# Spreading gate rows over the partitions by DMA instead of by a matmul and a copy

## What is computed

```python
def _more_forward(x, Wg, bg, W1, b1, W2, b2):
    cur = x
    for r in range(R):                                   # R = 4
        flat = cur.reshape(-1, h)                        # 1024 x 128
        logits = flat @ Wg[r] + bg[r]                    # 1024 x 4
        vals, idx = jax.lax.top_k(logits, TOPK)          # TOPK = 2
        w = jax.nn.softmax(vals, axis=-1)
        cw = jnp.sum(jax.nn.one_hot(idx, E, dtype=flat.dtype) * w[..., None], axis=1)
        hmid = jax.nn.gelu(jnp.einsum('nh,ehf->enf', flat, W1) + b1[:, None, :])
        y = jnp.einsum('enf,efh->enh', hmid, W2) + b2[:, None, :]
        out = jnp.einsum('ne,enh->nh', cw, y)
        cur = cur + out.reshape(b, s, h)
    return cur
```

## Time and profile before

| | |
|---|---|
| median of 3 runs | 539.47 us (538.99 to 543.11) |
| profiled execution, its own time | 534.68 us |
| its span (first to last instruction) | 532.9 us |
| granted TensorE clock over the span | 0.935 |
| busy PE, DVE, ACT, POOL | 462.3, 351.4, 323.8, 133.1 us |
| ACT's two gelus of a chunk (L665, L666), 128 each | 702 and 677 ns |
| DVE's split of a chunk (L1063), 128 | 688 ns |
| DMA traffic, mean | 30 GB/s |

### The profile page before, as it was taken

How to read it: one execution, slowest core, us unless ns; L and a number is a source line. 1 busy time by engine, 2 the same in 40 slices (tenths; PEclk the granted TensorE clock), 3 DMA queues, 4 the chain that set the end, 5 groups by cost and what they waited for, 6 DMA issues and landing times.

```text
span 532.9 us, 8485 instructions
## 1 busy us (share of the span) xinstructions
PE 462.3 (87%) x2692; PEld 354.8 (67%) x2692; DVE 351.4 (66%) x967; ACT 323.8 (61%) x620; POOL 133.1 (25%) x195
## 2 busy tenths in 40 slices
PE   3768998988994798579998877999999999999995
PEld 2447776755741587447777755878788787878783
DVE  4376766777469665546778746858585867777653
ACT  2446666632255334034666537898988989898892
POOL 7070000112145200123645330021111221111121
PEclk9978999997898799856999987999999999999999
DMA  8911111000400000001111000000000000000001
GB/s 293 369 35 26 31 28 29 16 1 1 159 1 1 0 1 2 0 20 30 33 31 31 22 0 1 1 2 1 0 0 0 0 0 0 0 0 1 1 1 39
DMA packets 12754, 16.07 MB, mean 30 GB/s; under 512 B 4008, under 2 KB 11304, under 8 KB 12080
## 3 DMA queue, kind: packets, MB, share of 16 engines
q1 hardware_dynamic: 12288, 14.79, 8.8%
q10 hardware_dynamic: 432, 0.85, 0.4%
HBM read 10.92 MB, written 0.52 MB: 21 GB/s over the span
## 4 chain that ended last, share of the span: by engine, by line
PE 57%; DVE 12%; issue 9%; ACT 8%; DMA 6%; SPq 5%; POOL 3%; ACTq 0%; POOLq 0%; DVEq 0%
SPq L295 5%; DMA bigr<-qk 5%; PE ps L1200 5%; PE ps L1515 4%; PE ps L1516 4%; PE ps L1514 4%; PE ps L1533 4%; PE ps L1532 4%; PE ps L1531 4%; PE ps L1245 3%; PE ps L1212 3%; POOL xnT L442 2%; ACT big L526 2%; PE ps L1522 2%; ACT qk L477 2%
## 5 line engine op out<-in xcount | busy, mean ns | idle before, releaser
L1063 DVE TENSOR_TENSOR bigr<-ps,bigr 128x512 fp32r<-128x512 f32 x128 | 86.2, 688 | 56.7 <-ACT ps L666 56.7
L526 ACT ACTIVATE big<-ps 128x512 f32<-128x512 f32 (+1 forms) x128 | 68.5, 547 | 58.2 <-PE ps L1212 56.1
L665 ACT ACTIVATE bigr<-ps,b 128x512 fp32r<-128x512 f32 x128 | 89.8, 702 | 3.0
L666 ACT ACTIVATE ps<-ps,b 128x512 f32<-128x512 f32 x128 | 86.6, 677 | 0.0
L442 POOL TENSOR_TENSOR xnT<-xnT,big 128x512 f32<-128x512 f32 x32 | 41.4, 1294 | 160.9 <-DVE big L1070 160.9
L1200 PE MATMUL ps<-bigr,qk 128*128 128x256 f32 (+1 forms) x224 | 55.1, 329 | 12.5 <-DMA bigr<-qk 11.1
L808 DVE TENSOR_REDUCE nmax<-ps 128x2 f32<-128x512 f32 x64 | 42.8, 688 | 18.4 <-PE ps L1200 17.6
L1212 PE MATMUL ps<-qk,bigr 128*128 128x256 f32 (+1 forms) x256 | 51.2, 285 | 1.0 <-ACT big L526 0.7
L1200 PEld LDWEIGHTS ps<-bigr,qk 128*128 128x128 f32 x224 | 35.7, 200 | 24.6 <-DMA bigr<-qk 15.0
L801 DVE CUSTOM_DVE_ANT_0 masked<-ps,later 128x128 f32<-128x128 f32 (+1 forms) x128 | 39.1, 352 | 18.8 <-PE ps L1200 18.7
L1514 PE MATMUL ps<-k1hi,w1hi 128*128 128x512 f32 x128 | 51.5, 402 | 0.0
(11 more groups left out here) (198 smaller groups left out, 852.6 us busy)
## 6 DMA issues: line engine op xcount, KB each, us to landing
bigr<-qk SPq DMA_DIRECT2D x128, 32.0 KB, 1.9
wi<-in_wi SPq DMA_DIRECT2D x1, 2048.0 KB, 7.7
wo<-in_wo SPq DMA_DIRECT2D x1, 2048.0 KB, 12.2
big<-in_sel SPq DMA_DIRECT2D x1, 1024.0 KB, 8.6
wo<-in_w SPq DMA_DIRECT2D x1, 1024.0 KB, 4.8
wi<-in_w SPq DMA_DIRECT2D x1, 1024.0 KB, 6.9
x<-in_x SPq DMA_DIRECT2D x1, 512.0 KB, 5.4
ctxT<-in_ctxT ACTq DMA_DIRECT2D x1, 512.0 KB, 5.2
```

The lines of the kernel that those rows point to most:

```text
L526: act.activation(prob[:, h % 8, c], ps[:, 2 + h % 2, c], ACT.Exp, scale=DH ** -0.5).then_inc(s(L + "_exp"), 1)
L665: act.activation(ghi[:, u % 2, c, :], ps[:, c, :], ACT.Gelu_apprx_tanh, bias=b1[:, u % E1, c:c + 1])
L666: act.activation(ps[:, c, :], ps[:, c, :], ACT.Gelu_apprx_tanh, bias=b1[:, u % E1, c:c + 1]).then_inc(s("ff1_gel"), 1)
L1063: v.tensor_tensor(glo[:, u % 2, c, :], ps[:, c, :], ghi[:, u % 2, c, :].bitcast(f32), ALU.subtract).then_inc(s("ff1_glo"), 1)
```

## The change

`cwT` becomes a plain f32 tile on 4 partitions, one for each expert. The matmul `spread` with its selector (`sel_er`, `sel_e`) and the copy `spread_weights` are gone; so are the three DVE instructions that rounded and split the gates, and the transposes take `cw` itself. In their place SP waits, for each half in each round, until ACT has written the four rows to `cwT`, and issues four DMAs. Each reads one row of 512 f32 (2 KB) on one partition 128 times, and writes it to the 128 partitions of `cwb[:, u, :]`: 256 KB a DMA, 4 a half, 8 halves, 32 in all. `combine` waits for the DMA of its own unit (semaphores `ff1_cwb0` to `ff1_cwb7`). What PE waits for at u = 3 and u = 7 stays.

```diff
-        cwT = sb("cwT", [P, 2, HALF], f32r)
-        sel_er = sb("sel_er", [P, E1, P], f32r)
+        cwT = sb("cwT", [E1, 2, HALF])
...
+            for Hf in range(2 * R1):
+                sp.wait_ge(s("ff1_ctev"), 1 + Hf + 1)
+                for e in range(E1):
+                    u = Hf % 2 * E1 + e
+                    sp.dma_start(cwb[:, u, :], cwT[e:e + 1, Hf % 2, :].unsqueeze(1).broadcast_to([1, P, HALF])
+                                 ).then_inc(s("ff1_cwb%d" % u), 16)
...
-            def spread_weights(U, u):
-
-                act.wait_ge(s("ff1_bcd"), U + 1)
-                act.activation(cwb[:, u % 8, :], ps[:, 6, :], ACT.Copy).then_inc(s("ff1_cwb"), 1)
...
-                act.activation(cwT[0:2 * E1, hf, :], ps[0:2 * E1, bank, :], ACT.Copy).then_inc(s("ff1_ctev"), 1)
+                act.activation(cwT[:, hf, :], ps[0:E1, bank, :], ACT.Copy).then_inc(s("ff1_ctev"), 1)
...
-                own.step(v.scalar_tensor_tensor(cw[:, 0:m], dif[:, 0:m], 1.0, selh[:, 0:m], ALU.add, ALU.mult))
-                own.step(v.tensor_copy(cwr[:, 0:m], cw[:, 0:m]))
-                c3, r3 = (a[:, 0:m].rearrange("p (n e) -> p n e", e=E1) for a in (cw, cwr))
-                own.mark(v.tensor_copy(cwhl[:, :, 0:E1], r3.bitcast(f32)))
-                v.tensor_tensor(cwhl[:, :, E1:2 * E1], c3, r3.bitcast(f32), ALU.subtract).then_inc(s("ff1_cwd"), 1)
+                v.scalar_tensor_tensor(cw[:, 0:m], dif[:, 0:m], 1.0, selh[:, 0:m], ALU.add, ALU.mult
+                                       ).then_inc(s("ff1_cwd"), 1)
...
-            def combine(U, u):
+            def combine(U, u, r):
                 dve.wait_ge(s("ff1_dn"), 2 + U + 1)
-                dve.wait_ge(s("ff1_cwb"), 1 + U + 1)
+                dve.wait_ge(s("ff1_cwb%d" % u), 16 * (r + 1))
...
-                    last = pe.transpose(ps[0:2 * E1, bank, n * P:n * P + P], cwhl[:, n, :], ident[:, :])
+                    last = pe.transpose(ps[0:E1, bank, n * P:n * P + P], cw[:, n * E1:n * E1 + E1], ident[:, :])
...
-            def spread(U, u):
-
-                u = u % (2 * E1)
-                pe.wait_ge(s("ff1_cwb"), U + 1)
-                pe.matmul(ps[:, 6, :], sel_er[:, u % E1, :], cwT[:, u // E1, :], start=True, stop=True
-                          ).then_inc(s("ff1_bcd"), 1)
```

More of the change, by code:

```diff
@@ L195, in decoder_kernel @@
         cw = sb("cw", [P, NT * E0])
-        cwr = sb("cwr", [P, NT * E0], f32r)
-        cwhl = sb("cwhl", [P, 4, 2 * E1])
-        sel_e = sb("sel_e", [2 * E1, E1, P])
         oNT = sb("oNT", [P, TPB, P])
@@ L283, in _ @@
             load("ff1", tie1[:, :, :], w["tie1"].partition_broadcast(P))
-            load("ff1", sel_e[:, :, :], w["sel_e"])
             load("ff0", wi0[:, :, :, :], w["wi0"])
@@ L325, in _ @@
             pool.wait_ge(s("const"), 6)
-            pool.memset(cwT[:, :, :].bitcast(f32), 0.0).then_inc(s("ff1_zero"), 1)
-            pool.memset(sel_er[:, :, :].bitcast(f32), 0.0).then_inc(s("ff1_zero"), 1)
             pool.memset(first_row[:, :], 0.0).then_inc(s("at1_row"), 1)
@@ L454, in _ @@
             act.sem_inc(s("ff1_ctev"), 1)
-            act.sem_inc(s("ff1_cwb"), 1)
             for name, dst, src in (("ctx", ctxT[:, :], "ctxT"), ("ctx", wctx[:, :, :], "wctx"),
@@ L684, in round_ @@
                     if not (last and u == 7):
-                        spread_weights(U0 + u + 1, u + 1)
                         gelus(U0 + u + 1, u + 1)
@@ L693, in _ @@
             gelus(0, 0)
-            act.wait_ge(s("ff1_zero"), 2)
             gate_rows(0, 0, 6)
             evacuate_xnT("ff1", 1, 5)
-            spread_weights(0, 0)
             with act.Fori(0, R1 - 1) as r:
@@ L1017, in constants @@
             def constants():
-                dve.wait_ge(s("ld_ff1"), 6 * 16)
-                dve.wait_ge(s("ff1_zero"), 2)
-                own.mark(v.tensor_copy(sel_er[0:2 * E1, :, :], sel_e[:, :, :]))
+                dve.wait_ge(s("ld_ff1"), 5 * 16)
                 own.mark(v.tensor_scalar(maskf[:, :], mask_i[:, :], 0, None, ALU.not_equal))
@@ L1095, in round_ @@
                         add_experts(0)
-                    combine(U0 + u, u)
+                    combine(U0 + u, u, r)
                     if u == 0:
@@ L1106, in _ @@
             dve.wait_ge(s("ln_xnT"), ln("ff1", 2) + 2)
-            per = 2 * 1 + 2 * (9 + 3)
+            per = 2 * 1 + 2 * 9
             with dve.Fori(0, R1 - 1) as r:
@@ L1488, in gate_rows @@
                 for n in range(4):
-                    last = pe.transpose(ps[0:2 * E1, bank, n * P:n * P + P], cwhl[:, n, :], ident[:, :])
+                    last = pe.transpose(ps[0:E1, bank, n * P:n * P + P], cw[:, n * E1:n * E1 + E1], ident[:, :])
                 last.then_inc(s("ff1_ct"), 1)
             def first_logits():
-                pe.wait_ge(s("ld_ff1"), 6 * 16)
+                pe.wait_ge(s("ld_ff1"), 5 * 16)
                 pe.wait_ge(s("ln_xnT"), ln("ff1", 2) + 1)
@@ L1554, in round_ @@
                     if not (last and u == 7):
-                        spread(U0 + u + 1, u + 1)
                         up(U0 + u + 1, u + 1)
@@ L1575, in _ @@
             pe.wait_ge(s("ff1_ctev"), 2)
-            spread(0, 0)
             pe.wait_ge(s("xa1_res"), TPB + TPB * B)
@@ L1615, in shape_constants @@
         c[n] = (np.arange(E)[None, :] < np.arange(E)[:, None]).astype(f)
-    c["sel_e"] = np.ascontiguousarray(np.broadcast_to(
-        (np.arange(2 * E1)[:, None] % E1 == np.arange(E1)[None, :])[:, :, None], (2 * E1, E1, P))).astype(f)
     return c
```

## The result

The changed kernel takes 652.23 us in the median of 4 runs (649.43 to 654.87), against 540.96 us for the kernel before in the same comparison; the ratio is 1.2055, with a 95% interval of 1.1974 to 1.2136. The forecast was 656 us, range 610 to 748. The profiled execution took 649.43 us, its span is 647.7 us.

The account below looks back on a forecast made before the run. PE bounds the last stage before, the new DMAs after: first rows 329.98, issue 0.59, start and completion 1.9, 32 x 9.7 = 310.4, tail 6.2, outside 1.8, median 4.8 give 655.7, predicted 656 us (range 610 to 748).

Parts of the forecast that it names:

- What bounds the kernel: Last stage: PE is the bound, busy 119.96 of 120 us at full clock, while the DMA engines move nothing.
- the DMA's price: Each new 256 KB DMA reads one partition at 26.9 GB/s, so it takes 9.7 us.
- the halved rate of the key copies: SBUF copies between 32 partitions: 14.6 to 15.1 GB/s per engine, about half the loads' rate, suggesting two engines share one way.
- the bound from below: For one new DMA's time: the store of x moves the same 256 KB from 128 partitions, landing in 2.3 us.
- The queue is always full: SP's queue in the last stage: four DMAs take 38.8 us against PE's 23.7 a half, so 32 run gapless, 310 us.
- The sum: Whole kernel: last landing at 642.9, span 649.1, with 1.8 us outside 650.9, plus 4.8 for the median: 655.7 us.
- The clock: PE in the last stage: clock may fall to 0.5, giving 678 us; a mixture off the path expected; chance 0.12.
- SP's issue: SP's queue: about 0.59 us to issue a DMA, 2.4 us for four; landings about 12, 21, 31, 41 us.
- What the removal brings: PE loses 32 matmuls: 1.1 us a half, 8.2 us over thirty slots, plus 1.1 in the prologue, 9.3 us together.
- the rival "hidden": Last stage: DMAs under 5.9 us each are hidden, leaving only removed work; 530 us, 1.7% faster; chance 0.12.

Follow-up runs that it names:

- the kernel with no spreading: Against the kernel before: spreading DMAs and semaphores left out, combine multiplies with a constant weight tile; 536.04 us, ratio 0.9946; in a second comparison 534.58 us, 0.9900.
- rows on 32 partitions: The change, but each gate row stands on 32 partitions, each read four times by the DMA; 536.22 us, ratio 0.9923 to the kernel before.
- 4 apart: The change, but each DMA reads four partitions lying 4 apart (32e, +4, +8, +12); 537.16 us, ratio 0.9923 to the kernel before.
- through HBM: The change, but SP writes the four rows to an HBM buffer and reads them from there; 536.18 us, ratio 0.9903 to the kernel before.
- 64 destinations: The change, but each DMA writes only 64 of the 128 destination partitions; 534.33 us, ratio 0.9872 to the kernel before.
- the 8 matmuls in the gap: Eight matmuls into unused bank 4 before up(1), added to the 32-partition kernel (533.90 us, 0.9852; again 534.84, 0.9894) and the kernel without spreading (533.22 us, 0.9839).

## Why the prediction was right, and where it was off

**What bounds the kernel, and the DMA's price: right, and shown.** The step that decided was the price of one DMA that reads one partition. I put it at 9.7 us; it is 9.6 to 9.8. The row that pointed to it, the halved rate of the key copies, did point to the right thing: with the way to a group of partitions as the narrow place, four neighbours stay slow, and four that lie apart do not; and an engine moves 24.5 GB/s where each has a group of its own, but 14.4 where sixteen read 32 partitions, which are eight such groups. The figure itself was a choice between rows: by 29.2 GB/s it would have been 9.0 us and 633 us in all, by 20.8 12.6 us and 748, and no row showed that 26.9 was the one to take. To that extent the closeness of the number is luck; the mechanism is not. The store's 2.3 us, the bound from below, is of the order of what a DMA takes once it reads 32 partitions or HBM (landings of 4.8 and 3.8 us with four issued together).

**The queue is always full: right.** The DMA share is 0.90 through the stage and the units stand 9.59 to 9.82 us apart without an exception at the halves' seams, the last one aside.

**The sum: right to 1.5 us on the profiled execution** (650.9 against 649.43). Its terms: the first rows were ready at 330.3 + 0.57 = 330.9 (330.0 assumed); the first `combine` began at 342.78 (342.2 by the prediction's terms); 31 steps make 298.2 us, where 31 x 9.7 would be 300.7; from the last `combine` to the end of the span 647.7 - 640.97 = 6.7 us (6.2 assumed; the four transposes take 1.11 us now, at a granted clock of 0.50, in place of 0.66 at 1.00); 1.7 us outside. The errors are small, and they partly cancel.

**The clock: right as put.** It is granted at 0.86 in the window, a mixture as forecast, and it isn't on the path. The pitch is 0.43 us behind the wait of 3.65 us shown above; behind a wait of 1.46 us, before the matmul at 363.45, it stays at 0.23. With the matmuls stretched in this way PE is busy 75% of the window (89.80 of 120 us), not 60%.

**SP's issue: wrong, with no effect.** I said 0.59 us each, and landings that grow to 41 us within a group. The issues take 9.59 us in the median, and the landings stay at 32.7 us: an issue takes as long as a transfer, so SP seems to be held until one of those ahead is through, with 32.7 / 9.6 = 3.4 under way in the mean. Nothing else waits on that queue here but the stores.

**What the removal brings: mis-sized.** The term was 8.2 + 1.1 = 9.3 us. Shown: 0.81 us a half in place of 1.1, so 6.1 us over 7.5 halves; and in the prologue 0.9 us lost where 1.1 were to be gained. For the halves I had priced the slots at 0.25 and 0.34 us, yet the changeover behind logits and gate rows stays and falls on the next matmul. In the kernel with no spreading the first matmul behind the gate rows has it:

```profile
357.25 0.40 PE L1517 MATMUL ps<-bigr,w2hi 128*128 128x512 f32 x1
357.75 0.49 PE L1504 MATMUL ps<-k1hi,w1hi 128*128 128x512 f32 x1
358.08 0.39 PE L1505 MATMUL ps<-k1hi,w1lo 128*128 128x512 f32 x1
```

Its slot is 0.33 us. The wait for the gate rows in front of it has grown too, from 350.22 - 349.82 = 0.40 us to 0.50 us between starts. Four times the plain pitch of 0.233, less this 0.1, is 0.83. For the prologue I had counted the gap as free time and not asked what the matmuls in it do for the clock. On this change the term is of no account. It would have mattered for the rival "hidden": the kernels whose transfers are hidden (rows on 32 partitions, 4 apart, through HBM, 64 destinations) are 0.8 to 1.3% faster, not 1.7%.

**A version that beats both.** Rows on 32 partitions with the 8 matmuls in the gap: 0.9852 and 0.9894 of the time before, in two comparisons. It leaves the gates in f32 without rounding and splitting them, as the change does, and its time can't be told from that of the kernel with no spreading and the same 8 matmuls.

## What to carry to other kernels

A transfer is to be priced by the narrowest place that all its bytes pass, not by its size and the number of DMA engines: idle DMA engines say nothing if every byte comes from one partition. If a row must go to all partitions, spread its copies over partitions that do not lie next to each other before the DMA, or take it from HBM. And where a matmul is removed from a stretch in which PE waits, look at the pitch of the matmuls behind the gap: the removed ones may have kept the clock up.

## What the runs showed of the hardware

- One partition of SBUF, read by sixteen DMA engines at a share of 0.90, gives 27.2 GB/s (9.63 us for 256 KB from 400 to 439 us; 27.0 in the mean of thirty steps); read for 96 destinations it gives 27.1.
- One group of four neighbouring partitions, read by four engines, gives 24 to 25 GB/s together. In the kernel whose rows stand on four such groups the rate also rises to 50 to 57 for stretches.
- Four partitions that lie 4 apart, again read by four engines, give 98 GB/s, 24.5 for each engine. Thirty-two partitions, read by sixteen engines, give 216, 14.4 for each; such a transfer lands 4.8 us after issue, four being issued together.
- One row in HBM, read 128 times, lands 3.8 us after issue, four being issued together.
- An issue on SP's queue takes 0.54 us at the shortest and 9.59 us in the median, as long as a transfer, with three or four such transfers pending.
- In the gap before `up(1)`, after a wait of 2.64 to 2.92 us on PE the matmuls followed at a pitch of 0.43 us, the 1.2 GHz level; after waits of 1.89 and 0.69 us with a matmul between them they followed at 0.23.
